# Attention in two rounds of four key tiles: a score bank lent to the projections, maxima fills moved behind scores

## What is computed

```python
def _L0_attn_ref(X, Wq, Wk, Wv, Wpost):
    Q = (X @ Wq).reshape(n, s, NUM_HEADS, KEY_WIDTH)
    K = (X @ Wk).reshape(n, s, NUM_HEADS, KEY_WIDTH)
    V = (X @ Wv).reshape(n, s, NUM_HEADS, VALUE_WIDTH)
    raw_attn = jnp.einsum('bshe,bthe->bsth', Q, K * inv_sqrt_d)
    attn = jax.nn.softmax(raw_attn, axis=2)
    A = jnp.einsum('bsth,bthe->bshe', attn, V).reshape(n, s, NUM_HEADS * VALUE_WIDTH)
    A = jax.nn.gelu(A, approximate=False)
    return X + A @ Wpost
...
x = L0_attn_X
xn = _layernorm(x, axis=-1)
s = _L0_attn_ref(xn, L0_attn_Wq, L0_attn_Wk, L0_attn_Wv, L0_attn_Wpost)
g = _silu(_L0_ffn_ref(xn, L0_ffn_weight, L0_ffn_bias))
x = x + s * g
```

## Time and profile before

| | us |
|---|---|
| median of 3 runs | 1503.74 |
| lowest and highest | 1503.32, 1508.24 |
| the profiled execution | 1504.28 |
| its span, first to last instruction | 1502.5 |
| PE busy | 1456.3 |
| POOL busy | 1144.7 |
| DVE busy | 1080.7 |
| ACT busy | 804.7 |
| PE's share of the chain that ended last | 88% |

### The profile page before, as it was taken

One profiled execution on the slowest core, in us unless ns is written; L12 is line 12 of the kernel. 1 busy time (PEld: TensorE's weight loads), 2 busy tenths in 40 slices (PEclk: granted clock), 3 DMA queues, 4 the chain that ended last, 5 costly groups with the idle time before them and its releaser, 6 DMA issues.

```text
span 1502.5 us, 25748 instructions
## 1 busy us (share of the span) xinstructions
PE 1456.3 (97%) x10369; PEld 794.2 (53%) x10369; DVE 1080.7 (72%) x1408; ACT 804.7 (54%) x1123; POOL 1144.7 (76%) x545
## 2 busy tenths in 40 slices
PE   5999999999999999999999999999999999999988
PEld 2555455555555555555555554555555555555478
DVE  6577777777777777777777777777777777777632
ACT  3455564555556565455555655555555555555563
POOL 0778788878887887887888778788778878877930
PEclk9999999999999999999999999999999999999999
DMA  2000000000000000000000000000000000002361
GB/s 76 1 8 15 8 15 29 16 8 15 15 8 15 15 13 24 15 14 8 15 15 15 8 15 14 9 15 15 8 15 8 1 1 1 1 1 80 118 220 49
DMA packets 25589, 35.40 MB, mean 24 GB/s; under 512 B 1792, under 2 KB 15872, under 8 KB 25472
## 3 DMA queue, kind: packets, MB, share of 16 engines
q1 hardware_dynamic: 25472, 33.76, 6.4%
HBM read 19.07 MB, written 14.68 MB: 22 GB/s over the span
## 4 chain that ended last, share of the span: by engine, by line
PE 88%; DVE 10%; issue 1%; ACT 1%; DMA 0%; POOL 0%; SPq 0%; ACTq 0%
PE acc L397 26%; PE scores L384 21%; PE peaks L368 11%; PE extra L287 8%; PE scores L388 7%; DVE half_maxes L807 5%; PE extra L317 4%; PE extra L300 4%; PE scores L456 4%; PE extra L324 2%; PE extra L338 1%; DVE extra L782 1%; DVE extra L783 1%; DVE extra L784 1%; DVE quant L785 1%
## 5 line engine op out<-in xcount | busy, mean ns | idle before, releaser
L696 POOL TENSOR_TENSOR prob_sum<-prob_sum,probs 128x1024 f32<-128x1024 f32 x384 | 912.1, 2375 | 236.7 <-ACT probs L571 209.3
L807 DVE TENSOR_REDUCE half_maxes<-peaks 128x2 f32<-128x1024 f32 x504 | 611.5, 1213 | 282.4 <-PE peaks L368 281.2
L571 ACT ACTIVATE probs<-scores 128x1024 f32<-128x1024 f32 x512 | 497.2, 1023 | 385.3 <-PE scores L388 375.4
L397 PE MATMUL acc<-probs,vals 128*64 128x512 f32 x2048 | 487.9, 597 | 0.0
L397 PEld LDWEIGHTS acc<-probs,vals 128*64 128x64 f32 x2048 | 137.2, 137 | 246.3 <-issue 218.1
L823 DVE RECIPROCAL inv_sum<-inv_sum 128x128 f32<-128x128 f32 x256 | 240.1, 941 | 0.0
L368 PE MATMUL peaks<-k_hi,q_hi 64*128 64x512 f32 x1008 | 226.0, 443 | 0.0
L384 PE MATMUL scores<-q_hi,k_hi 64*128 64x512 f32 x1024 | 202.7, 392 | 0.0
L388 PE MATMUL scores<-max_rows,ones_r 64*128 64x512 f32 x1024 | 202.2, 390 | 0.0
L384 PE MATMUL scores<-q_hi,k_lo 64*128 64x512 f32 x1024 | 202.1, 390 | 0.0
L384 PE MATMUL scores<-q_lo,k_hi 64*128 64x512 f32 x1024 | 202.0, 390 | 0.0
(11 more groups left out here) (147 smaller groups left out, 1025.6 us busy)
## 6 DMA issues: line engine op xcount, KB each, us to landing
att_scratch<-att SPq DMA_DIRECT2D x48, 256.0 KB, 2.0
probs<-att_scratch SPq DMA_DIRECT2D x8, 512.0 KB, 9.1
xTs<-att_scratch SPq DMA_DIRECT2D x4, 512.0 KB, 7.9
out_dram<-xn SPq DMA_DIRECT2D x8, 256.0 KB, 4.1
x_in<-in_L_attn_X SPq DMA_DIRECT2D x3, 512.0 KB, 4.0
q_hi_back<-att_scratch SPq DMA_DIRECT2D x2, 512.0 KB, 4.2
q_lo_back<-att_scratch SPq DMA_DIRECT2D x2, 512.0 KB, 5.0
k_hi_back<-att_scratch SPq DMA_DIRECT2D x2, 512.0 KB, 6.6
```

What stands on the lines that cost most here:

```text
L397: last = mm(acc[own[h], :], vals[(s // 2) % 2][:, j, own[h]], probs[j][:, h, :], start=(j == 0), stop=(j == KT - 1), tile_position=col[h])
L571: sa.activation(probs[j][:, :, :], scores[j % 2][:, :, :], ACT.Exp, scale=DH ** -0.5).then_inc(probs_ready, 1)
L696: gp.tensor_tensor(prob_sum[s % 2][:, :, :], before[:, :, :], probs[j][:, :, :], ALU.add).then_inc(probs_summed, 1)
L807: v.tensor_reduce(half_maxes[:, :, f // 2, f % 2], peaks[:, :, :], AX.X, ALU.max).then_inc(peaks_read, 1)
```

## The change

A step now has two rounds of four key tiles. The row stretch of round r is `score(4r)`, `peak(4r)`, `score(4r+1)`, `score(4r+2)`, `peak(4r+1)`, `score(4r+3)`, `peak(4r+2)`, `peak(4r+3)`; the column stretch has four `weigh`, of the four tiles before, and the fills. Fill f = 4r+2 of the maxima goes to `scores[0]`, which the exp of tile 4r+2 must have read; fill 4r+3 goes to `peaks` again, and waits for the reduction of 4r+1 only.

The halves of q, k, v, and the transposes w and x, no longer go to `extra`. They are lent the two banks of `scores[1]` in the middle of a column stretch, after the exp of tile 4r+3, and are read before `score(4r+5)` (semaphores `lent_filled`, `lent_read`). `extra` keeps den, turn, turn_x, ffn and the rounding.

On ACT four exps stand together, and the copies behind them. On DVE four reductions stand together; the rounding is in round 0 of an odd step, in one piece; the reciprocals are of the step before from round 0 on; `spread_rows` is the last of round 1. Work for the next batch (centring, squares, roots, scaling) moves to other rounds, part of the scaling to round 0 of a later step.

```diff
-                for r in range(4):
+                for r in (0, 1):
                     before, behind = extras(s, r)
-                    if s + 1 < NS:
-                        peak(s + 1, 2 * r)
-                    score(s, 2 * r)
-                    score(s, 2 * r + 1)
-                    if s + 1 < NS:
-                        peak(s + 1, 2 * r + 1)
+                    peaks_here = (lambda f: peak(s + 1, 4 * r + f)) if s + 1 < NS else (lambda f: None)
+                    late = [(s, j) for j in range(4)] if r == 1 else [(s - 1, j) for j in range(4, 8)] if s > 0 else []
+                    score(s, 4 * r)
+                    peaks_here(0)
+                    score(s, 4 * r + 1)
+                    score(s, 4 * r + 2)
+                    peaks_here(1)
+                    score(s, 4 * r + 3)
+                    peaks_here(2)
+                    peaks_here(3)
                     for use in before:
                         run(use)
-                    if r > 0:
-                        weigh(s, 2 * r - 2)
-                        weigh(s, 2 * r - 1)
-                    elif s > 0:
-                        weigh(s - 1, 6)
-                        weigh(s - 1, 7)
+                    for at in late[:2]:
+                        weigh(*at)
+                    if lent(s, r):
+                        pe.wait_ge(probs_ready, 8 * s + 4 * r + 4)
+                    for use in lent(s, r):
+                        run(use)
+                    for at in late[2:]:
+                        weigh(*at)
                     for use in behind:
                         run(use)
...
-                above(pe, peaks_read, 8 * s + f)
+
+                place = scores[0] if f % 4 == 2 else peaks
+                if f % 4 == 2:
+                    pe.wait_ge(probs_ready, 8 * (s - 1) + f + 1)
+                elif f % 4 == 3:
+                    pe.wait_ge(peaks_read, 8 * s + f - 1)
+                else:
+                    pe.wait_ge(peaks_read, 8 * s + f)
...
-                if j == 0 and s == 0:
-                    pe.wait_ge(peaks_read, 8)
+                if j == 0:
+                    pe.wait_ge(peaks_read, 8 * s + 8)
+                if j == 4 and s + 1 < NS:
+                    pe.wait_ge(peaks_read, 8 * s + 11)
+                if j % 4 == 1:
+                    above(pe, lent_read, lent_up_to[2 * s + j // 4])
```

More of the change, by code:

```diff
@@ L36, in extras, with lent @@
         before, behind = [], []
-        if half == 0:
[L38 to L59, removed]
+        if r == 0:
+            if s > 0:
+                before.append(("den", s - 1))
+            if half == 1:
+                before.append(("quant", n))
+            elif n > 0:
+                behind.append(("turn_x", n - 1))
+        else:
+            if half == 0 and n > 0:
+                before.append(("ffn", n - 1))
+            if s + 1 < NS:
+                behind.append(("turn", s + 1))
+        return before, behind
+    def lent(s, r):
+        n, half = s // 2, s % 2
+        if half == 0:
+            return [("qk"[r], n + 1, 0), ("qk"[r], n + 1, 1)] if n + 1 < NP else []
+        if r == 0:
+            return [("v", n + 1, 0), ("v", n + 1, 1)] if n + 1 < NP else []
+        if n == 0:
+            return [("w",)]
+        if n % HP == 4 and n // HP + 1 < B:
+            return [("x", n // HP + 1, 0), ("x", n // HP + 1, 1)]
+        return []
     FILLS = [("v", 0, 0), ("v", 0, 1), ("turn", 0)]
+    LENT = []
     for s in range(NS):
-        for r in range(4):
+        for r in (0, 1):
             for part in extras(s, r):
                 FILLS += part
+            LENT += lent(s, r)
     FILLS += [("den", NS - 1), ("turn_x", NP - 1), ("ffn", NP - 1)]
@@ L538, in copy_xT_later @@
                 is_filled(act, use)
-                sa.copy(xT[b][:, halves[half]], bank(use)).then_inc(extra_read, 1)
+                sa.copy(xT[b][:, halves[half]], bank(use)).then_inc(lent_read, 1)
             def high(use):
@@ new lines, in _ @@
+                for r in (0, 1):
+                    for j in range(4 * r, 4 * r + 4):
+                        exps(s, j)
+                    if r == 0 and s > 0:
+                        copy_sums(s - 1)
+                    if r == 0 and half == 1:
+                        unscale(n)
+                    if half == 0 and ahead:
+                        high(("qk"[r], n + 1, 0))
+                        high(("qk"[r], n + 1, 1))
+                    if half == 1 and r == 0 and ahead:
+                        copy_v(("v", n + 1, 0))
+                        copy_v(("v", n + 1, 1))
+                    if half == 1 and r == 1 and n == 0:
+                        copy_square(("w",), ffn_wT)
+                    if half == 1 and r == 1 and n % HP == 4 and later < B:
+                        copy_xT_later(("x", later, 0))
+                        copy_xT_later(("x", later, 1))
+                    if r == 0 and s > 0:
+                        copy_acc(s - 1)
+                    if r == 0 and half == 0 and n > 0:
+                        copy_square(("turn_x", n - 1), quant_T)
+                    if half == 0 and r == 1 and n % HP == 1 and n > 1:
@@ L857, in _ @@
                 next_step, ahead, later = s + 1 < NS, n + 1 < NP, n // HP + 1
[L858 to L878 removed]
+                for r in (0, 1):
+                    if r == 0 and s > 1:
+                        invert(s - 2, 3)
+                    if r == 1 and s > 0:
+                        invert(s - 1, 1)
+                    if next_step:
+                        for f in range(4 * r, 4 * r + 4):
+                            reduce_peaks(s + 1, f)
+                    if r == 1 and next_step:
+                        join_maxima(s + 1)
+                    if s > 0:
+                        invert(s - 1, 2 * r)
+                    if r == 1 and half == 0 and n > 0:
+                        gate_argument(n - 1)
+                    if half == 0 and ahead:
+                        low(("qk"[r], n + 1, 0))
+                        low(("qk"[r], n + 1, 1))
+                    if half == 1 and r == 0:
+                        quantise_tile(n, 0)
+                        quantise_tile(n, 1)
+                    if s == 0 and r == 0:
```

104 lines of the change are left out of this document (46 added, 58 removed).

## The result

The changed kernel takes 1537.26 us (median of 4 runs, 1535.07 to 1538.90) against 1503.67 before: by the ratio of all their runs 1.0214 times as long, 95% interval 1.0200 to 1.0228. The forecast was 1537.

A forecast was written before the change was run, and what follows sets the result against it. PE, busy for 97% of the span, was taken as the bound. -45 - 24 + 88 + 11 + 3 = +33 on the profiled 1504.28 gave 1537.3, with the median 0.5 below: forecast 1537 us, 8-in-10 range 1502 to 1553.

The forecast's parts named there:

- Trips, -45: PE's changes from rows to columns and back: four a step become two, 128 fewer at 0.35 us, -45 us.
- The turn's wait, -24: PE's wait for DVE before the turn of the maxima goes, as the rounding leaves the place before their join: -24 us.
- Waits in a stretch, +88: PE's row stretches wait for exps and reductions and restart slowly: 0.70 us in each of 126 stretches, +88 us.
- The estimate of 0.58 a stretch: Stretch loss by the skill page's isolated-matmul latency, 0.58 instead of 0.70 us; the sum some 15 us lower.
- The spread, +11: Fourth pair of a step's first score tile waits for DVE's spread maxima and restarts: 0.17 x 63, +11 us.
- ACT's work for the next batch, +3: ACT's scaling of rows now stands in front of an exp in up to six places: 0 to 9 us, taken as +3.
- What was costed at nothing: Lent fills waiting for tile 3's exp (cover 1.5 us) and POOL's sums (cover 1.6 us): no cost to PE.
- the second rival: POOL's sums come late and hold PE in the sum over keys: 1553 us; POOL or another late engine, chance 0.09.
- The first rival, 1500,: A wait within PE's row stretch costs only itself, without slow restart: loss 0.46 a stretch, 1500 us; chance 0.15.

The follow-up runs named there:

- trips_mid: The kernel before with 96 more trips between rows and columns, the first weigh moved between the two score tiles in some rounds; 1555.75 us.

## Why the prediction was right

- **Trips, -45.** Right. One added trip costs 0.36 in the rows and 0.37 over all 96 of `trips_mid`. The 0.39 to 0.43 by totals came from experiments that also moved waits.
- **The turn's wait, -24.** Right. In the kernel before, 38 turns of the loops start late, by 23.5 us in sum (start to start, beyond the 1.77 or 1.72 that the `weigh` takes); in the changed kernel none of 63 does. Taking most of this wait away alone in the kernel before gave -17, with 10 late turns and 7.7 us left.
- **Waits in a stretch, +88.** Right in sum and in its parts: a median of 5.51 against 5.49 for a second stretch, starts within 0.03 us, and three kernels with shorter exps and reductions within 5 us of the same layout. The one assumption in it without a row was that a held pair starts again with 0.34. It holds wherever the next pair is free to start: behind all 126 held tiles 2 and all 63 held fourth pairs from step 1 on (0.33 to 0.34), and behind fill 2 in the kernel with short reductions (0.34). Behind fill 2 of the changed kernel itself the wait for the reduction hides it. The same order without these waits (short exps and reductions) has 0.23 behind tile 2 and behind fill 2, so it is the wait and not the place. The estimate of 0.58 a stretch, which the prediction set beside its row, did not come: the second stretches lose 0.71.
- **The spread, +11.** The step was right: 0.16 a step in the trace (10 us), and 8 us in the total.
- **ACT's work for the next batch, +3.** The term came out at 5.6 us, inside the 0 to 9 of the prediction, but was priced on the wrong work. I had priced the scaling of rows, which moves ahead of an exp: it lengthens three stretches by 0.42 (5.93 against 5.51), 1.3 us. The roots, of which I said that they stood in front of an exp before too, lengthen three by 0.39, 1.2 us. The largest delay is the gate's silu, with two loads of tables, which now stands directly in front of a step's first exp, 3.1 us in three stretches. In the kernel before no stretch of 10 pairs is longer than 2.55, against 2.51 on average, so none of this cost PE anything there. ACT's timeline at the silu, and PE's tile 2 behind it:

```profile
817.97 1.28 ACT L566 ACT_TABLE_LOAD   x1
819.26 1.06 ACT L566 ACTIVATE gate<-gate 128x1024 f32<-128x1024 f32 x1
820.34 1.28 ACT L615 ACT_TABLE_LOAD   x1
821.63 1.94 ACT L615 ACTIVATE probs<-scores 128x1024 f32<-128x1024 f32 x2
```

```profile
819.18 0.50 PE L420 MATMUL scores<-q_hi,k_hi 64*128 64x512 f32 x2
...
822.71 0.50 PE L420 MATMUL scores<-q_hi,k_hi 64*128 64x512 f32 x2 [1.00 <-ACT probs L615]
```

  Tile 2 starts 3.53 into its stretch instead of 2.48 (776.93 less 774.45 in an ordinary first stretch). Such a tile 2 is 1.05 us late, and the silu comes once for each of three batches.
- **What was costed at nothing.** POOL is nowhere in the view of waits as what PE waits for; the second rival, 1553 and more, did not come. The lent fills wait for an exp in a single place, 0.2 us (0.5 for its weight load).
- **What was not in the sum.** The first stretch of step 0 took 7.34 instead of 5.67: from 34 to 36 us the granted clock was 0.63 of full speed and from 36 to 38 us 0.52, so for most of that time it was the 1.2 GHz level, and pairs stand 0.43 apart there. In the kernel before it was 1.00. PE had stood 1.6 us before the first turn in both kernels; why the clock fell in the one is open. It costs 1.7 us.
- **The first rival, 1500,** fell on the row 765.31 to 765.65 and its like. The Trainium skill (TensorEngine Tiling (Array Packing), section "Key Properties") ties a drain to a change of tiling mode. The traces show a loss of 0.35 a trip there, and also 0.11 on a held pair in the same mode, so a rule about mode changes alone would have left out a third of what a stretch loses (0.23 of 0.69).

Trips at 0.37 make -47, the turn -24, and all stretches together, with the spread, ACT's work and the slower clock in step 0, +107 instead of +102: +36, against 34.5 in the span. Small differences in step 0, the last step and the tail, which I did not take apart, make up the rest. The mechanism is shown; that the forecast hit to the microsecond is luck, since the errors of the terms partly cancel and the runs of the changed kernel alone lie 4 us apart. The totals of the experiments on single terms came within 5 us, with the exception of the two with added trips, which moved waits besides.

## What to carry to other kernels

When PE is the bound and two ping-pong buffers feed it, lay the stretch out by start times, with hand-overs, before merging rounds: merging saves a fixed price at each border (0.35 us here), but waits that were a round away move into the stretch, and each that PE reaches costs its length plus a slow restart (0.11 here). Look for what stands between the last two links of a chain that PE waits for: moving three small vector operations gave 1.1%, in a kernel where the larger rearrangement lost 2.1%.

## What the runs showed of the hardware

A matmul pair that was held by a semaphore costs 0.11 us more than the wait, in the same tiling mode (0.34 to the next pair instead of 0.23, 765.31 to 765.65, and so behind all 126 held tiles 2). But a weight load that starts 0.11 ahead of its matmul's turn costs nothing (34.37 and 34.48); in the changed kernel's trace 103 pairs from step 1 on have their load 0.10 to 0.14 ahead, and they and the next pair stand 0.22 to 0.25 apart. So here a release had to come some 0.1 us before the matmul was due, and not at its time, to be free.
